# Cross attention and routed experts on one core: scores moved between the two halves of the transposes, exponents one tile later, ratios spread by transfers

## The reference, cut to what matters

```python
def _L0_xattn_ref(Q, K, V, Wq, bq, Wk, bk, Wv, bv, Wo, bo):   # B=128, S=64, D=128
    q = _split_heads(Q @ Wq.T + bq, B, S)
    k = _split_heads(K @ Wk.T + bk, B, S)
    v = _split_heads(V @ Wv.T + bv, B, S)
    scores = jnp.einsum('bhqd,bhkd->bhqk', q, k) * scale
    probs = jax.nn.softmax(scores, axis=-1)
    out = jnp.einsum('bhqk,bhkd->bhqd', probs, v)
    return out.transpose(0, 2, 1, 3).reshape(B, S, D) @ Wo.T + bo
def _L0_ffn_ref(x, Wr, br, W1, b1, W2, b2):
    expert_idx = jnp.argmax(xf @ Wr.T + br, axis=-1)
    h = jax.nn.relu(jnp.einsum('td,efd->etf', xf, W1) + b1[:, None, :])
    y = jnp.einsum('etf,edf->etd', h, W2) + b2[:, None, :]
    return y[expert_idx, jnp.arange(xf.shape[0])]
x = x + _L0_xattn_ref(_layernorm(x), ctx_1024, ctx_1024, ...)
x = x + _L0_ffn_ref(_layernorm(x), ...)
```

## Time and profile before

| | |
|---|---|
| median of 3 runs | 495.99 us |
| profiled execution: time, span | 498.64 us, 496.8 us |
| busy: TensorE, its weight loads | 460.0 us (93%), 348.5 us (70%) |
| busy: VectorE, ScalarE, GpSimd | 408.5 (82%), 312.9 (63%), 240.6 us (48%) |
| costliest on VectorE | maximum 64 x 1222 ns, subtraction 64 x 1209 ns |
| DMA | 33.98 MB, mean 68 GB/s |

### The profile page before, as it was taken

The page is one execution under the profiler, slowest core; times in us unless marked ns, Lnnn a source line. Parts: engine busy times, 40 slices in busy tenths (PEclk is TensorE's granted clock), DMA queues, the critical chain, the costliest instruction groups (busy, mean ns, idle before and its releaser), DMA issues. The chain is left out here.

```text
span 496.8 us, 18730 instructions
## 1 busy us (share of the span) xinstructions
PE 460.0 (93%) x6467; PEld 348.5 (70%) x6467; DVE 408.5 (82%) x1061; ACT 312.9 (63%) x589; POOL 240.6 (48%) x390
## 2 busy tenths in 40 slices
PE   2999988899999999999999999989789999999990
PEld 1666644466666666666666666678779999999990
DVE  4999876677899998998989999956788878888870
ACT  1677776656666666666666666555557777777760
POOL 0548621222242554644645546355757654545451
PEclk9999999999999999999999999997999999999996
DMA  8356300001100111111111118432323332222100
GB/s 282 112 145 177 90 13 18 18 17 20 21 19 17 39 39 35 35 33 36 37 35 34 34 45 314 147 92 61 80 53 111 95 87 66 71 62 75 40 29 0
DMA packets 32752, 33.98 MB, mean 68 GB/s; under 512 B 6675, under 2 KB 26006, under 8 KB 32416
## 3 DMA queue, kind: packets, MB, share of 16 engines
q1 hardware_dynamic: 27840, 24.10, 18.6%
q0 software_dynamic: 4832, 8.80, 5.4%
HBM read 19.14 MB, written 9.99 MB: 59 GB/s over the span
## 5 line engine op out<-in xcount | busy, mean ns | idle before, releaser
L451 POOL TENSOR_TENSOR VP<-BIG,C 128x128 f32<-128x128 f32 x128 | 56.0, 457 | 131.1 <-PE PS L1020 125.1
L929 PEld LDWEIGHTS PS<-C,SB 128*128 128x128 f32 x512 | 53.7, 140 | 65.4 <-ACT SB L549 33.2
L701 DVE TENSOR_REDUCE MX<-PS 128x16 f32<-128x1024 f32 x64 | 78.2, 1222 | 23.4 <-PE PS L881 22.0
L473 POOL DMA_INDIRECT out<-SB,BIG x71 | 70.0, 986 | 52.7 <-DVE SB L854 44.4
L929 PE MATMUL PS<-C,SB 128*128 128x128 f32 x512 | 83.8, 286 | 6.3 <-ACT PT L532 5.3
L549 ACT ACTIVATE SB<-SB 128x1024 f32<-128x1024 f32 x64 | 67.6, 1057 | 20.5 <-DVE SB L709 18.9
L1041 PE MATMUL PS<-BIG,KM 128*128 128x128 f32 x568 | 78.6, 281 | 0.2
L709 DVE TENSOR_TENSOR SB<-PS,MX 128x1024 f32<-128x1024 f32 x64 | 77.4, 1209 | 1.7
L1054 PE MATMUL PS<-KM,SB 128*128 x568 | 75.7, 277 | 0.6 <-ACT SB L566 0.6
L466 POOL DMA_INDIRECT rows<-X,DESTI x64 | 64.3, 1004 | 19.6 <-issue 13.5
L1041 PEld LDWEIGHTS PS<-BIG,KM 128*128 128x128 f32 x568 | 71.4, 196 | 1.3 <-issue 1.1
(11 more groups left out here) (122 smaller groups left out, 699.7 us busy)
## 6 DMA issues: line engine op xcount, KB each, us to landing
BIG<-rows SPq DMA_DIRECT2D x71, 66.0 KB, 2.0
X<-in_x SPq DMA_DIRECT2D x16, 256.0 KB, 3.3
PT<-in_ctxT SPq DMA_DIRECT2D x16, 256.0 KB, 2.9
KM<-BIG SPq DMA_DIRECT2D x240, 16.0 KB
BIG<-in_we SPq DMA_DIRECT2D x1, 2576.0 KB, 10.4
KM<-in_w SPq DMA_DIRECT2D x1, 2048.0 KB
out<-SB,BIG POOLq DMA_INDIRECT x71, 2.3
rows<-X,DESTI POOLq DMA_INDIRECT x64, 2.5
```

The source lines that it names most:

```text
L451: last = nc.gpsimd.tensor_tensor(dst, v, own, ALU.mult)
L473: nc.gpsimd.indirect_dma_start(out=out, out_offset=bass.IndirectOffsetOnAxis(ap=RT[:, s.r, ID:ID + 1].bitcast(i32), axis=0), in_=YO[:, s.r ...
L701: nc.vector.tensor_reduce(MX[:, n % 2, :], sc, axis=AX.X, op=ALU.max).then_inc(mx_done, 1)
L929: last = nc.tensor.transpose(bank(4)[:, i * P:(i + 1) * P], SB[:, (n + 2) % 3, hp * P:(hp + 1) * P], ident)
```

## The change: what it does

- TensorE's step is reordered: transposes of X, first half of tile n-2's transposes, scores of tile n, second half, projection (now tile n-10), logits, ranking, values and denominators.
- ScalarE does the exponents of tile n-1 between the two copies of step n, where it did those of tile n at its end; the copy of X's transposes stands ahead of the first copy.
- VectorE takes the reciprocal ahead of the maximum. `L_MUL`, `L_X1` and what follows lag one step more, `M_SEED` does not; `SOON` becomes 0.
- The spreading matmul and its selection matrix (256 KB of the constants) go. SyncE writes the reciprocals to HBM and reads them back spread over the channels into RDX; VectorE multiplies from there.
- Keys and queries get another channel order (ScalarE turns WQ and WK at the start), so KM takes 8 transfers of 16 partitions a group.
- The experts' weights are fetched from ScalarE's queue, behind its steps 58 and 61, and TensorE waits for W2 at the third block only.

```diff
-L_MUL = 8
-L_X1 = 9
+L_MUL = 9
+L_X1 = 10
 M_BN = L_X1 + 1
 M_MOM = M_BN + ST - 1
 M_SEED = 18
...
-M_TR = L_X1 + 2
+M_TR = L_X1 + 3
...
-SOON = 2
+SOON = 0
...
+            def ratios(g):
+                sp.wait_ge(rd_done, g + 1)
+                need(sp, rdx_in[g % 2], 16 * (g // 2))
+                sp.dma_start(ratio[g % 2], RD[:, g % 2, :]).then_inc(rd_out[g % 2], 16)
+                need(sp, ot_ready, GT * (g - 1))
+                sp.wait_ge(rd_out[g % 2], 16 * (g // 2 + 1))
+                of = ratio[g % 2].rearrange("(h a) q -> h a q", a=DK)[:, 0:GT, :].rearrange("h t q -> h (t q)")
+                sp.dma_start(RDX[:, g % 2].rearrange("p t q -> p (t q)"), of.unsqueeze(1).to_broadcast([H, DK, GT * P])).then_inc(rdx_in[g % 2], 16)
+
+            for s in range(1, NG):
+                sp.wait_ge(q_kept, s + 1)
...
+                for j in range(HP):
+                    sp.dma_start(KM[j:P:HP, s % 2, j, :], KT[j:P:HP, s * GW:(s + 1) * GW]).then_inc(km_in[s % 2], 16)
+                if s >= 2:
+                    ratios(s - 2)
...
+            ratios(NG - 2)
             sp.wait_ge(padr_in, 16)
...
             for n in range(NB1 - E):
+                if n == 8:
+                    ratios(NG - 1)
                 load_block(0)(Step(n // RR, n % RR, RR))
...
+            for k, w in enumerate((WQ, WK)):
+                last = nc.scalar.copy(RDX[:, 0, k, :].rearrange("p (g d j) -> p g d j", g=2, d=DK), turned(w))
...
+                if 1 <= n < NT + 1:
+                    act.wait_ge(sub_done, n)
+                    nc.scalar.activation(SB[:, (n + 1) % 3, :], SB[:, (n + 1) % 3, :], ACT.Exp, scale=SCALE).then_inc(exp_done, 1)
                 if 2 <= n < NT + 2:
                     act.wait_ge(pt_done, 2 * (n - 2) + 2)
...
+                if late == 0 and 0 <= g < NG:
+                    dve.wait_ge(od_done, GT * g + GT)
+                    need(dve, rdx_in[g % 2], 16 * (g // 2))
+                    nc.vector.reciprocal(RD[:, g % 2, :], bank(5)[:, P * (g % 2):P * (g % 2) + P]).then_inc(rd_done, 1)
                 if n < NT:
                     dve.wait_ge(s_done, n + 1)
...
+                    dve.wait_ge(rdx_in[g % 2], 16 * (g // 2 + 1))
+                    nc.vector.tensor_tensor(OT[:, m % 2, :], RDX[:, g % 2, t, :], NUM[:, m % 8, :], ALU.mult).then_inc(ot_ready, 1)
...
+                    need(pe, sub_done, n - 1)
+                    scores(n)
+                m = n - 2
+                if 0 <= m < NT:
                     pe.wait_ge(pt_ready, 2 * m + 1)
                     transposes(m, 1)
```

More of the change, by code:

```diff
@@ L406, in stage1 @@
                 if 8 <= n < 12:
[L407 to L410, removed]
+                    for j in range(2 * (n - 8), 2 * (n - 7)):
+                        pool.dma_start(KM[j:P:HP, 0, j, :], KT[j:P:HP, 0:GW]).then_inc(km_first, 16)
             for n in range(NG):
@@ L890, in stage1 @@
                 need(pe, k_kept, s.n - 1)
-                nc.tensor.matmul(bank(4 + s.r % 2), WK, CT[:, s.r, :], start=True, stop=True).then_inc(k_done, 1)
+                nc.tensor.matmul(bank(4 + s.r % 2), RDX[:, 0, 1, :], CT[:, s.r, :], start=True, stop=True).then_inc(k_done, 1)
                 pe.wait_ge(xn_done, s.n + 1)
@@ L974, in stage2 @@
-                j = s.routing(M_RANK)
-                if j is not None:
-                    pe.wait_ge(hot_done, j + 1)
-                    sums = bank(7)[:, RK:RK + (ST + 1) * E]
-                    nc.tensor.matmul(sums, COUNT[:, 0, :], HOT[:].rearrange("p t e -> p (t e)"), start=True, stop=False)
-                    for t in range(ST):
-                        last = nc.tensor.matmul(sums[:, (t + 1) * E:].rearrange("p (t e) -> p t e", e=E), COUNT[:, 1, :],
-                                                HOT[:, t:t + 1, :].to_broadcast([P, ST - t, E]), start=False, stop=t == ST - 1)
-                    last.then_inc(rank_done, 1)
@@ new lines, in stage2 @@
+                m = n - L_X1
+                if 0 <= m < NT:
+                    nc.tensor.matmul(bank(7)[:, P:2 * P], OT[:, m % 2, :], WO, start=True, stop=True).then_inc(wo_done, 1)
+                for i in range(4):
+                    j = s.batch(M_LG + 2 * i)
+                    if j is not None:
+                        pe.wait_ge(x1t_ready, 4 * j + i + 1)
+                        for t in range(2):
+                            at = 2 * P + (ST * (j % 2) + 2 * i + t) * E
+                            last = nc.tensor.matmul(bank(7)[:, at:at + E], X1T[:, i % 2, t, :], WR, start=True, stop=True)
+                        last.then_inc(lgp_done, 1)
@@ new lines, in stage2 @@
+                j = s.routing(M_RANK)
+                if j is not None:
+                    pe.wait_ge(hot_done, j + 1)
+                    sums = bank(7)[:, RK:RK + (ST + 1) * E]
+                    nc.tensor.matmul(sums, COUNT[:, 0, :], HOT[:].rearrange("p t e -> p (t e)"), start=True, stop=False)
+                    for t in range(ST):
+                        last = nc.tensor.matmul(sums[:, (t + 1) * E:].rearrange("p (t e) -> p t e", e=E), COUNT[:, 1, :],
+                                                HOT[:, t:t + 1, :].to_broadcast([P, ST - t, E]), start=False, stop=t == ST - 1)
+                    last.then_inc(rank_done, 1)
```

135 lines of the change are left out of this document (57 added, 78 removed).

## The result

The changed kernel takes **502.67 us** (median of 4 runs, 502.32 to 503.06), the kernel before 495.85 (4 runs, 495.64 to 498.73): ratio 1.0113, 95% interval 1.0069 to 1.0156. Run again beside each other they took 502.27 (6 runs) and 497.07 (11 runs), ratio 1.0111 (1.0083 to 1.0139). Slower by 1.1%. The profiled execution of the changed kernel took 503.06 us, span 501.3.

What follows compares the result with a forecast made beforehand. TensorE's own order was taken to set the step, 3.96 us. Terms summed to +3.0: 501.6 us from the profiled 498.64, and 499.0 by the median of 495.99; range 487 to 505.

Steps and rivals of the forecast that it cites:

- Ramp, -4.5: Steps before tile 13: the step falls from 3.96 to 3.22 us, 3.41 with projection; 4.5 us gained in all.
- Start, 0: Kernel start: smaller constants, added small transfers and reordering copies lie beside the wait for W and x; 0 (-0.7 to +0.9).
- Steps 13 to 56, +2.8: Middle steps: 3.41 us odd to even, 4.48 even to odd, plus five stacks with ranking; 175.4 us against 172.6.
- the number wait: TensorE's transposes of X, opening odd steps, wait for the numerator copy: 0.47 us in every second step.
- the stack: VectorE's moments, seed and reciprocal fall together before the next maximum; TensorE waits 1.02 us once in 8 steps.
- 56 to 63, +0.9: Steps from tile 56 to 63: VectorE's table work for the experts stays, one more stack; 30.5 us against 29.57.
- 63 to the first block, +0.3: Scores of tile 63 to first expert block, 14.96 us before: between -2.1 and +1.4, taken as +0.3.
- Last group's ratios, +3.0: Third expert block: VectorE waits 3 us (2.7 to 4.0) for group 15's ratios, queued on SyncE behind eight block loads.
- Expert weights, +0.5: ScalarE issues the experts' weights behind step 58, between numerator copies TensorE waits for: +0.5 us (0 to 1.4).
- The extra change of the tiling mode: Even steps, logits to tiled matmuls: a skill's drain rule would add 0.15 in 25 steps, 3.8 us; left uncharged.
- The rival of the clock: Expert blocks 2 to 5: the last group's wait causes a second half-clock stretch, +3.5, 503.5 us; chance 0.22.
- The rival of the dissolved waits: Odd steps' waits vanish, the step goes towards VectorE's floor of 3.70; halfway, at 3.90, 487 us; chance 0.30.

Runs made afterwards that it cites:

- experiment 1: The changed kernel run again unchanged, beside the kernel before: 502.27 us, ratio 1.0111.
- experiment 6: The changed kernel with the two small bias transfers issued by ScalarE instead of SyncE: 500.24 us, ratio 1.0073 to the kernel before.
- experiment 5: The changed kernel with the seed of the inverse root one step later than the moments (M_SEED 19): 511.27 us, ratio 1.0284 to the kernel before.
- experiment 3: The changed kernel with X's transposes behind the scores and ScalarE's copy of them behind the exponents: 493.94 us, ratio 0.9941 to the kernel before.
- experiment 2: The changed kernel with the last group's ratios issued behind four block loads instead of eight: 496.47 us, ratio 0.9985 to the kernel before.
- experiment 9: The changed kernel with 14 idle matmuls in the four steps that interleave with the first expert blocks: 503.11 us, ratio 1.0126 to the kernel before.
- experiment 4: The changed kernel with the spreading matmul back and no transfers of ratios, new order kept: 504.05 us, ratio 1.0144 to the kernel before.

## Why the prediction was right in its sum, and where its median was not

The forecast sum of +3.0 us was made against the profiled execution of before and gives 501.6 us; the comparable execution of the changed kernel (experiment 1) took 501.99. That the sum came out so near is partly luck: four terms together came out 3.9 us lower than forecast; two others, and a loss in the expert blocks that I had not counted, 4.5 us higher. Term by term, from those two profiles:

- **Ramp, -4.5.** The scores of tile 13 come 3.60 earlier although the first come 0.89 later: -4.5. The step of 3.22 is there (83.86 to 93.50 in three).
- **Start, 0.** It is +0.9, the upper end (experiment 6 gives it back): the two bias transfers take SyncE 1.44 us.
- **Steps 13 to 56, +2.8.** Measured +1.0. The pieces are right: 3.44 and 4.46 for 3.41 and 4.48, ranking 0.24 for 0.25, the number wait in each odd step. The step of the sum that failed is the stack, 0.66 (0.43 and 0.23) for 1.02. The first 0.43 is a wait that I had not worked out, of the denominators for the reciprocal (0.39 in the row at 203.40); the second, for X1, is 0.21. I had added moments (1.27) and seed (0.96) from rows of the kernel before; here they take 1.76 together (200.15 to 202.39, less 0.48). The stacking is not the reason: apart, in experiment 5, the same operations take 0.80 and 0.81, no more than in the stack (0.91 and 0.82). In the rows of before single ones of them took 0.36, 0.43 and 0.33 us, here 0.24, 0.16 and 0.17; why is open. Experiment 3 shows that the wait in each odd step was the large term of the stage: without it a pair of steps is 7.44 instead of 7.90, and the stage 7.0 us shorter.
- **56 to 63, +0.9:** +0.3. The sum had a slip of its own: four of the seven steps go from even to odd, so the pieces give 28.15 and not 27.6, and the term would have been 1.4. Part of the miss is again the stack; the rest is not parted.
- **63 to the first block, +0.3:** -0.7, inside its bounds.
- **Last group's ratios, +3.0:** 4.2 by experiment 2, a little over the upper bound of 4.0. What was longer than counted is the queue ahead: SyncE reached the ratios 19.8 us after the scores of tile 63 (315.61 to 335.42), where I had 17.9. VectorE stood ready 19.6 us after them (340.43 less the idle of 5.26), inside my 19.2 to 20.6. The two transfers took 5.0 from issue to use; I had 5.8 from the scattered rows in one place and 5.3 in the sum (17.9 to 23.2). The Trainium skill, "DMA: Bandwidth & Descriptors", Anatomy of one DMA — SWDGE (gpsimd) path, gives a fixed cost of about 2.0 us for a transfer, which it measured on GpSimd's queue; my estimate from it was 4.5. On SyncE's queue here they landed in 1.6 and 3.2 us (64 and 256 KB), so that its price is about as near as the row's.
- **Expert weights, +0.5:** no sign of it. Instead the blocks lose 2.4 us from block 0 to the last beyond the wait, in experiments 1 and 2 alike (block 0 3.1 and 3.2 us ahead of before, the last 3.6 behind and 0.8 ahead). Some 1.6 of it is lost by block 7. From there the lag to before swings, as I read it because the routing falls beside other blocks (3.1 us less by block 9, 2.8 more by 12, 0.8 less by 14, 1.8 more by 17), for 0.7 in all. I had held that what SOON = 0 moves behind the first blocks was paid in any case. That is read from block starts and not tried, and the cause is open.
- **The extra change of the tiling mode:** no idle shows between the logits and the tiled matmuls, and even to odd is 4.46 without a charge. The rule weighed in the prediction (the Trainium skill, "TensorEngine Tiling (Array Packing)", Tiling Modes) would, by the estimate made there, add 0.15 to that. At this change the trace does not show it; at the changes from transposes to scores and from denominators to transposes 0.17 and 0.20 us of idle stand in the rows.

**The median** is where it went otherwise: 502.67 against the forecast 499.0, inside the range of 487 to 505, and +6.8 us, not +3.0. In the larger sample beside experiment 1 it is +5.2 (502.27 and 497.07): the 6.8 has also to do with how few executions of before it rests on. By the yardstick of 0.992, before ran at full clock in its faster executions (beside experiment 1, 495.65 to 496.03 us at 0.992 in five of eleven; 498.5 and more at 0.984, as in both profiles), while none of the ten executions of the changed kernel was above 0.986. At a span of 500 us, 0.007 of the mean is 3.5 us. The step that failed is taking the difference between two profiled executions over to the median: by the mean clocks the stretch at half clock in the earlier trace rows belongs to some executions of before, and one like it to each of the changed kernel. No profile of before at 0.992 was caught, so this is argued and not shown. The rival of the clock, "+3.5, with the wait at 4.0: 503.5", names what seems to have decided the median, at 0.22; its "second such stretch" is wrong for the profiles, where the stretch moved and there was one in each, but fits the typical execution.

What brings the clock down is not shown. With the wait of 3.8 us the mean was at most 0.986 in 26 of 27 executions (the first four, and experiments 1, 3, 6 and 9). Without it, it was at most 0.987 in six of twelve (experiment 2), and 0.991 to 0.993 in all five of experiment 4, which has no transfers of ratios but one more matmul in each step. So the wait makes the stretch nearly certain, and it is not its only cause.

The rival of the dissolved waits is refuted by the 0.65 in the rows; experiment 3 shows what it would have been worth.

## What to carry to other kernels

When a dependency becomes a transfer, count where its last instance stands in the queue of the engine that issues it: fifteen of sixteen were free here, and the last, behind eight loads, took back most of what the removed matmuls gave. When work is moved within an in-order engine, look at what its first instruction now waits for; two transposes moved behind the scores, with their copy, were worth 7 us in 43 steps. And before a difference of half a per cent is taken from one profile, compare its mean granted clock with that of the other runs.

## What the runs showed of the hardware that was not expected

- The mean granted clock sorts executions of one kernel: beside experiment 1, the kernel before had 0.992 at 495.65 to 496.03 us, 0.987 and 0.988 at 497.1 to 497.5, 0.984 at 498.5 to 499.2. It does not fix the time: beside experiments 2 and 9, 0.992 stood at up to 497.01 and 496.83 us.
- The same idle of 2.57 us was followed by half clock in one of the twelve profiles in which it stands (74 to 77 us) and by full clock in the others.
- VectorE's multiply of 128x128 took 368 ns on average with both operands in SBUF (64 of them, 226 to 578; first profile after) and 279 with one in PSUM (64, 226 to 293; profile before).
- Ten small VectorE operations in a row (200.66 to 202.39) start 0.08 to 0.21 us apart. The same operation can take 0.16 us in one kernel and 0.43 in the other (the third of the moments, 128x8, in each batch from 160 to 280 us), which no run here explains.
